# Where VectorE copies a pass's sums, in a cross-attention and expert kernel on one core

## The chip, the cores and the metric

The kernel runs on one core of one Trainium2 chip. The metric is the device time of one execution in microseconds (us), and the figure that is compared is the median over several runs. Five engines take part, each with its own in-order program: TensorE (PE in the rows, its weight loads PEld), VectorE (DVE), ScalarE (ACT), GpSimd (POOL) and SyncE (SP). They meet through semaphores: one instruction adds to a semaphore when it is done, and another engine's program waits until the semaphore has reached a number.

## The reference

Only the first half of the layer touches the change. `x` has 1024 tokens of 128 channels, `ctx` has 6404 rows of 96 channels, and there are 16 heads of 8 channels.

```python
q = layernorm(x) @ Wq + bq          # 1024 x 128
k = ctx @ Wk + bk;  v = ctx @ Wv + bv   # 6404 x 128
attn = softmax(clip(q_h @ k_h.T * scale))       # per head, 1024 x 6404
x = x + concat_h(attn @ v_h) @ Wo + bo
x = x + alpha * gelu(ln(x) @ W1m + b1m) @ W2m + (1 - alpha) * (two of eight experts, gated)
```

The softmax is taken without subtracting a maximum where a bound computed early in the kernel says that this is safe, and this branch is the one that runs.

## The kernel before, in words

**Passes and tiles.** The attention is cut into 8 passes. Pass `p` has 4 heads (`g`) and one half of the queries (512 of them). For every block of 128 context rows (`kt`, 0 to 49, and a short tail, 50) TensorE makes 4 score matmuls, one for each head, each 128 x 512 (L1143; the tail's is L1138). Three such chunks make a tile of 1536 columns in PSUM (`ps[t % 2]`), and ScalarE takes the exponential of a tile in one instruction (L533). There are 500 tiles. A finished block is multiplied with the values and a column of ones, and summed in a PSUM bank that the pass owns, `po[p % 2]` (L1228, the tail's L1214). Each of those 4 matmuls is two instructions in the trace, so a block is "x8" there.

**VectorE's share of the exponentials.** 27 blocks don't go to ScalarE. Their 108 chunks of scores go into the other bank, `po[1 - p % 2]`, as "spare jobs" of TensorE between two tiles (`spare_job`), at the tiles that `D_PLAN` names, and VectorE computes their exponential with a polynomial. For each chunk it runs L840 (round, into `du`) and L843 (the fraction, into `df`), which also frees the bank (`spare_taken`). For each pair of chunks it runs six steps, called stages in `pair_until`: stage 1 is L859, 2 is L868 (with a small L866 before it in some pairs), 3 is L870, 4 is L873, 5 is L876 and 6 is L879, which adds to `d_ready`. The stages of a pair run interleaved with the two chunks of the pair that follows: after the first of them up to stage 3, after the second up to stage 6. A block that is ready is summed at its own tile (the last number of a `D_PLAN` row).

**The end of a pass.** When the last block of pass `i` is summed, VectorE copies the bank to `oraw` (`take_sums`, L822; in the rows this is a COPY into region_kT, of which `oraw` is a part). A few tiles later TensorE transposes the copy, 4 blocks of 128 columns, back into the bank just freed: this is the spare job "tokens" (L1181). VectorE then normalises (`normalise`, L814 and L815) and adds to `spare_taken`. Every spare job waits until `spare_taken` has counted all jobs before it (L1159), so the chunk that follows "tokens" waits for `normalise`.

**What sets the order.** VectorE's program follows the list `SPARE`, the spare jobs in order of their tile. The "tokens" jobs stand at these tiles, with the score chunk ahead of each:

```
pass that ends   last tile   chunk before, its number and tile   tokens   next chunk
0                65          8 (first of its pair), 64           67       71
1                127         24 (first), 126                     130      133
2                190         40 (first), 189                     193      196
3                250         55 (second), 249                    252      256
4                312         71 (second), 311                    315      318
5                375         87 (second), 374                    378      381
6                436         102 (first), 431                    441      477
```

TensorE's order around a tile `t` is: scores of tile `t + 2` (which wait for the exponential of tile `t`), then the spare job of tile `t`, if there is one, then the values of the blocks that tile `t` completed.

Of the kernel before, what the change touches and what calls it, by code (L numbers as in the profile page):

```python
# [135 lines left out]
for gap in EPI_GAPS:  # L136
# [9 lines left out]
SPARE = sorted([(t, "score", GH * d + k) for d, (_, _, at, _, _) in enumerate(D_PLAN) for k, t in enumerate(at)]  # L146
               + [(NORM_AT[p], "tokens", p) for p in range(NP - 1)] + [(t, "v", c) for c, t in V_AT.items()]
               + [(t, "bound", n) for n, t in enumerate(BOUND_TILES)]
               + [(GSUM_TILE, "gsum", 0), (ROWS_TILE, "rows", 0)])
# [24 lines left out]
def pass_at(t):  # L174

    return min(p for p in range(NP) if t <= PASS_END[p])


def pv_bank(p):
    return p % 2  # L180
# [7 lines left out]
def build(nc, x, ctx, wq, bq, wk, bk, wv, bv, wo, bo, alpha, w_gate, b_gate, w1m, b1m, w2m, b2m,  # L188
# [4 lines left out]
    with ExitStack() as stack:  # L193
# [383 lines left out]
        def _(dve):  # L577
# [187 lines left out]
            def first_half_main(link):  # L765

                take_first_attT()
                residual(0, po[EPI_BANK][:, :], link)
                dve.wait_ge(std_ready, 2)
                scale_rows(halves[0])  # L770
                dve.wait_ge(xnT_psum, NHALF + 1)
                v.tensor_copy(xnT[:, 0:BANK], po[EPI_BANK][:, :]).then_inc(xnT_ready, 1)
                dve.wait_ge(xnT_ready, NHALF + 1)
                link(v.tensor_reduce(msum[:, 0:1], xnT[:, 0:BANK], AX.X, ALU.add))
                for cb in range(CB):
                    dve.wait_ge(pre_psum, cb + 1)
                    v.tensor_scalar(pre[:, cb, :], po[EPI_BANK][:, :], b1T[:, E * CB + cb:E * CB + cb + 1], None,  # L777
                                    ALU.add).then_inc(pre_taken, 1)
# [11 lines left out]
            with dve.If(safe != 0):  # L790
# [17 lines left out]
                def normalise(p, tok):  # L808

                    g, half = PASSES[p]  # L810
                    tok4 = tok.rearrange("p (t j m) -> p t j m", j=GH, m=QUAD)
                    tiles = slice(halves[half].start, halves[half].stop)
                    n = tiles.stop - tiles.start
                    flink(v.reciprocal(rden[:, tiles, :], tok4[:, :, :, D]))  # L814
                    return v.tensor_tensor(att_tok[:, tiles, g * GH * D:(g + 1) * GH * D].rearrange("p t (j d) -> p t j d", j=GH),  # L815
                                           tok4[:, :, :, 0:D],
                                           rden[:, tiles, :].unsqueeze(3).broadcast_to([P, n, GH, D]), ALU.mult)

                def take_sums(p):

                    dve.wait_ge(pv_done, VALUES_OF_PASS[p][-1] + 1)
                    v.tensor_copy(oraw[:, p % 2, :], po[pv_bank(p)][:, :]).then_inc(o_taken, 1)  # L822
# [5 lines left out]
                def d_count(key, ins):  # L828

                    d_done[0] += 1  # L830
                    d_mark[key] = d_done[0]
                    ins.then_inc(d_step, 1)

                def split_exponent(c, n):

                    i, m = divmod(c, 2)
                    part = slice(m * BANK, (m + 1) * BANK)
                    src = po[1 - pv_bank(pass_at(SPARE[n][0]))][:, :]
                    dve.wait_ge(spare_psum, n + 1)
                    d_count(("u", c), v.tensor_scalar(du[:, i % 2, part], src, MAGIC, None, ALU.add))  # L840
                    pair_until(i - 1, 1 + 3 * m)
                    dve.wait_ge(d_step, d_mark["u", c])
                    v.scalar_tensor_tensor(df[:, i % 2, part], du[:, i % 2, part], MAGIC, src,  # L843
                                           ALU.subtract, ALU.subtract).then_inc(spare_taken, 1)
                    pair_until(i - 1, 3 + 3 * m)

                def pair_until(i, stage):

                    if i < 0:
                        return  # L850
                    u, f, q = du[:, i % 2, :], df[:, i % 2, :], dq[:, :]
                    d, half = divmod(i, 2)
                    res = dres[:, d % 2, half * 2 * BANK:(half + 1) * 2 * BANK]
                    while d_stage[i] < stage:
                        d_stage[i] += 1
                        if d_stage[i] == 1:
                            dve.wait_ge(d_step, d_mark["u", 2 * i + 1])
                            dve.wait_ge(spare_taken, SPARE_OF["score", 2 * i + 1] + 1)
                            d_count(("e", i), v.tensor_scalar(u.bitcast(U32), u.bitcast(U32), 23, None, ALU.logical_shift_left))  # L859
                        elif d_stage[i] == 2:  # L860
                            if d >= 2:
                                dve.wait_ge(pv_done, VALUES_OF_D[d - 2] + 1)
                            if half == 0:
                                p, kt = D_PLAN[d][0:2]
                                heads = slice(GH * PASSES[p][0], GH * (PASSES[p][0] + 1))
                                v.tensor_scalar(vd[:, d % 2, :].rearrange("p (h m) -> p h m", m=V9), v9[:, kt, heads, :],  # L866
                                                C5, None, ALU.mult)
                            d_count(("q1", i), v.scalar_tensor_tensor(res, f, A1, f, ALU.add, ALU.mult))  # L868
                        elif d_stage[i] == 3:
                            d_count(("q2", i), v.scalar_tensor_tensor(q, f, A2, f, ALU.add, ALU.mult))  # L870
                        elif d_stage[i] == 4:
                            dve.wait_ge(d_step, max(d_mark["q1", i], d_mark["e", i]))
                            d_count(("p1", i), v.scalar_tensor_tensor(res, res, B1, u, ALU.add, ALU.mult))  # L873
                        elif d_stage[i] == 5:
                            dve.wait_ge(d_step, max(d_mark["p1", i], d_mark["q2", i]))
                            d_count(("p2", i), v.scalar_tensor_tensor(res, q, B2, res, ALU.add, ALU.mult))  # L876
                        else:
                            dve.wait_ge(d_step, d_mark["p2", i])
                            v.scalar_tensor_tensor(res, f, R0, res, ALU.subtract, ALU.mult).then_inc(d_ready, 1)  # L879

                pairs = 0
                for n, (_, kind, i) in enumerate(SPARE):
                    if n < JOBS_V:
                        continue
                    if kind == "score":
                        split_exponent(i, n)
                        pairs = (i + 1) // 2
                        if pairs == len(d_stage):
                            pair_until(pairs - 1, 6)
                    else:  # L890
                        take_sums(i)
                        if pairs:
                            pair_until(pairs - 1, min(6, d_stage[pairs - 1] + BETWEEN))
                        dve.wait_ge(spare_psum, n + 1)
                        ins = normalise(i, po[1 - pv_bank(i + 1)][:, :])
                        ins.then_inc(spare_taken, 1)
                        if i == LAST_OF_HALF[0]:
                            first_half_main(flink)
# [111 lines left out]
        def _(pe):  # L1010
# [80 lines left out]
            def ffn_sum(t):  # L1091

                n = max(n for n, (t0, _) in enumerate(OUT_TILES) if t0 <= t)
                a = t - OUT_TILES[n][0]
                return [po[0], po[1], bank(4)][n][:, a * P:(a + 1) * P], a == 0
# [93 lines left out]
            def values_step(n):  # L1189
# [11 lines left out]
                if first and p >= 1:  # L1201
                    used = sum(at <= t for at, _, _ in SPARE)
                    if used:
                        pe.wait_ge(spare_taken, used)
                    if p >= 2:
                        pe.wait_ge(o_taken, p - 1)
# [188 lines left out]
```

## Time and profile before

| | |
|---|---|
| median of three runs | 789.02 us (788.52 to 789.54) |
| profiled execution, its own time | 791.65 us |
| its span, first to last instruction | 789.7 us |
| granted TensorE clock, mean | 0.991 of full |
| TensorE matmuls busy | 735.0 us (93%) |
| ScalarE busy | 718.7 us (91%) |
| VectorE busy | 564.1 us (71%) |

The rows below come from one profiled execution, and their times are counted from the span's start. In a timeline row the first number is the start, the second is how long the instruction or the merged run of like instructions took, then engine, line, operation, output<-input, shapes and count; what stands in brackets is how long the engine had been idle before it and who released it. Starts of following rows may lie a little before the end of the row ahead, since consecutive instructions of an engine overlap.

### The profile page before, as it was taken

The page shows a single profiled execution, that of the slowest core. Times are in us where ns is not written, and L with a number is a line of the kernel's source. Part 1 is how long each engine was busy: PE and PEld are TensorE (multiplying, and loading weights), DVE is VectorE, ACT ScalarE, POOL GpSimd, SP SyncE. Part 2 cuts the span into 40 slices and gives each one's busy share as a digit, 9 for nine tenths or more (in the row PEclk, how much of TensorE's full clock was granted, in tenths as well). Part 3 has the DMA queues.
Part 4 walks back from the last instruction along what each step waited for, and adds up shares of the span by engine and source line. Part 5 has one row for each costly group of instructions (what it writes and reads, how often), then busy time and mean ns, then how long its engine had stood idle before and what let it go on. Part 6 is the DMA issues. An engine that isn't in the chain of part 4 may idle for free.

```text
span 789.7 us, 13292 instructions
## 1 busy us (share of the span) xinstructions
PE 735.0 (93%) x5412; PEld 219.5 (28%) x5412; DVE 564.1 (71%) x789; ACT 718.7 (91%) x574; POOL 28.8 (4%) x50
## 2 busy tenths in 40 slices
PE   6999989999999999999989999999999999999898
PEld 3534322222222222222222222222222222222457
DVE  6944278798878978797778897897879782139320
ACT  4868999999999999999989999999999999999351
POOL 5240000000000000000000000000000000000000
PEclk9979999999999999999999999999999999999999
DMA  4678000011110000111100000111100000000010
GB/s 163 196 184 260 25 1 1 23 46 34 34 34 1 2 1 1 34 49 36 51 1 2 1 1 18 34 38 48 34 1 1 1 1 1 2 1 1 2 54 27
DMA packets 18043, 28.53 MB, mean 36 GB/s; under 512 B 5286, under 2 KB 8732, under 8 KB 17980
## 3 DMA queue, kind: packets, MB, share of 16 engines
q1 hardware_dynamic: 12730, 23.71, 10.1%
q0 software_dynamic: 4032, 3.30, 1.8%
q8 instruction: 45, 0.74, 0.4%
q10 hardware_dynamic: 1218, 0.64, 0.3%
q14 instruction: 18, 0.15, 0.1%
HBM read 19.50 MB, written 8.13 MB: 35 GB/s over the span
## 4 chain that ended last, share of the span: by engine, by line
PE 57%; ACT 19%; issue 16%; DVE 4%; DMA 2%; POOLq 0%; SPq 0%; POOL 0%; ACTq 0%
PE po L1228 30%; PE ps L1143 16%; ACT region_ctx L533 14%; ACT probs_own L533 5%; PE ps L1323 2%; PE po L1044 2%; PE po L1333 1%; DMA k_dram<-kparts 1%; PE ps L1033 1%; PE po L1214 1%; DVE pT L632 1%; DMA xres<-in_x 1%; PE po L1143 1%; PE po L1120 1%; DMA region_ctx<-in_w1e 0%
## 5 line engine op out<-in xcount | busy, mean ns | idle before, releaser
L533 ACT ACTIVATE region_ctx<-ps 128x1536 f32<-128x1536 f32 x375 | 528.4, 1509 | 14.1 <-PE ps L1143 13.7
L1228 PE MATMUL po<-region_ctx,v 128*9 128x512 f32 x2238 | 392.8, 598 | 0.5 <-ACT region_ctx L533 0.5
L1143 PE MATMUL ps<-qst,region_k 32*128 32x512 f32 x1492 | 251.4, 494 | 36.2 <-ACT region_ctx L533 25.9
L1143 PEld LDWEIGHTS ps<-qst,region_k 32*128 32x128 f32 x1492 | 96.6, 182 | 408.9 <-ACT region_ctx L533 288.8
L1228 PE MATMUL po<-probs_own,v 128*9 128x512 f32 x746 | 193.8, 602 | 0.5 <-ACT region_ctx L533 0.5
L533 ACT ACTIVATE probs_own<-ps 128x1536 f32<-128x1536 f32 x125 | 188.7, 1509 | 4.2 <-PE ps L1143 3.8
L840 DVE TENSOR_SCALAR region_kT<-po 128x512 f32<-128x512 f32 x108 | 74.1, 686 | 90.5 <-PE po L1143 90.5
L843 DVE SCALAR_TENSOR_TENSOR region_kT<-region_kT,po 128x512 f32<-128x512 f32 x108 | 73.5, 680 | 0.3
L879 DVE SCALAR_TENSOR_TENSOR dres<-region_kT,dres 128x1024 f32<-128x1024 f32 x54 | 66.1, 1225 | 1.7
L876 DVE SCALAR_TENSOR_TENSOR dres<-region_kT,dres 128x1024 f32<-128x1024 f32 x54 | 65.8, 1218 | 0.2
L868 DVE SCALAR_TENSOR_TENSOR dres<-region_kT 128x1024 f32<-128x1024 f32 x54 | 65.7, 1217 | 0.0
L870 DVE SCALAR_TENSOR_TENSOR region_kT<-region_kT 128x1024 f32<-128x1024 f32 x54 | 65.7, 1217 | 0.0
L873 DVE SCALAR_TENSOR_TENSOR dres<-dres,region_kT 128x1024 f32<-128x1024 f32 x54 | 65.6, 1214 | 0.0
L1228 PEld LDWEIGHTS po<-region_ctx,v 128*9 128x9 f32 x2238 | 42.3, 88 | 69.7 <-issue 66.0
L1143 PE MATMUL po<-qst,region_k 32*128 32x512 f32 x108 | 51.4, 476 | 0.0
L859 DVE TENSOR_SCALAR region_kT<-region_kT 128x1024 uint32<-128x1024 uint32 x54 | 36.9, 683 | 0.0
L672 DVE COPY v<-po 128x512 f32<-128x512 f32 (+1 forms) x13 | 8.8, 680 | 30.8 <-PE po L1044 30.8
L1228 PE MATMUL po<-dres,vd 128*9 128x512 f32 x216 | 28.2, 595 | 0.0
L486 POOL TENSOR_TENSOR rstd<-rstd,powers 128x4 f32<-128x4 f32 x2 | 2.1, 1028 | 688.0 <-DVE rstd L604 688.0
L1228 PEld LDWEIGHTS po<-probs_own,v 128*9 128x9 f32 x746 | 19.7, 88 | 23.5 <-issue 22.2
L1143 PEld LDWEIGHTS po<-qst,region_k 32*128 32x128 f32 x108 | 19.6, 181 | 1.2 <-issue 1.2
L777 DVE TENSOR_SCALAR region_ctxT<-po,b1T 128x512 f32<-128x512 f32 x4 | 3.0, 750 | 19.2 <-PE po L1120 19.2
(216 smaller groups left out, 352.8 us busy)
## 6 DMA issues: line engine op xcount, KB each, us to landing
region_k<-k_dram SPq DMA_DIRECT2D x40, 320.0 KB, 3.3
k_dram<-kparts SPq DMA_DIRECT2D x18, 320.0 KB, 4.5
qst<-q_dram POOLq DMA_DIRECT2D x12, 128.0 KB, 9.6
region_ctx<-in_ctx SPq DMA_DIRECT2D x2, 624.0 KB, 9.7
q_dram<-dres POOLq DMA_DIRECT2D x2, 512.0 KB, 3.1
k_dram<-kparts SPq DMA_DIRECT2D x2, 322.0 KB, 3.5
region_ctx<-in_ctx SPq DMA_DIRECT2D x1, 576.0 KB, 8.1
xres<-in_x SPq DMA_DIRECT2D x1, 512.0 KB, 4.6
```

Source lines behind the costliest of these rows:

```text
L533: act.activation(probs_of(t), ps[t % NSB][:, :], ACT.Exp, scale=ESCALE).then_inc(exp_ready, 1)
L840: d_count(("u", c), v.tensor_scalar(du[:, i % 2, part], src, MAGIC, None, ALU.add))
L843: v.scalar_tensor_tensor(df[:, i % 2, part], du[:, i % 2, part], MAGIC, src, ALU.subtract, ALU.subtract).then_inc(spare_taken, 1)
L859: d_count(("e", i), v.tensor_scalar(u.bitcast(U32), u.bitcast(U32), 23, None, ALU.logical_shift_left))
L868: d_count(("q1", i), v.scalar_tensor_tensor(res, f, A1, f, ALU.add, ALU.mult))
L870: d_count(("q2", i), v.scalar_tensor_tensor(q, f, A2, f, ALU.add, ALU.mult))
L873: d_count(("p1", i), v.scalar_tensor_tensor(res, res, B1, u, ALU.add, ALU.mult))
L876: d_count(("p2", i), v.scalar_tensor_tensor(res, q, B2, res, ALU.add, ALU.mult))
L879: v.scalar_tensor_tensor(res, f, R0, res, ALU.subtract, ALU.mult).then_inc(d_ready, 1)
L1044: last = mm(dst[:, (t % 4) * P:(t % 4 + 1) * P], lhsT, wv_sb[:, :], start=True, stop=True)
L1143: return mm(dst, kst[r, kt * P:(kt + 1) * P], qst[r, g, queries], start=True, stop=True)
L1228: last = mm(dst[QUAD * j:QUAD * j + V9, :], w, src, start=first, stop=last_one, skip_group_check=True)
```

## The change

`take_sums(i)` is called when VectorE's program reaches the "tokens" entry of `SPARE`. Before, the stages that belong behind the last chunk ahead of it (`pair_until` at the end of `split_exponent`) have been issued by then. After, `split_exponent` returns ahead of that call where the next entry is "tokens", and the "tokens" branch makes the same call after `take_sums`. So the copy moves ahead of some stages:

```diff
                     v.scalar_tensor_tensor(df[:, i % 2, part], du[:, i % 2, part], MAGIC, src,
                                            ALU.subtract, ALU.subtract).then_inc(spare_taken, 1)
+                    if SPARE[n + 1:n + 2] and SPARE[n + 1][1] == "tokens":
+                        return
                     pair_until(i - 1, 3 + 3 * m)
...
                     else:
                         take_sums(i)
+                        if SPARE[n - 1][1] == "score":
+                            pair_until(SPARE[n - 1][2] // 2 - 1, 3 + 3 * (SPARE[n - 1][2] % 2))
                         if pairs:
                             pair_until(pairs - 1, min(6, d_stage[pairs - 1] + BETWEEN))
                         dve.wait_ge(spare_psum, n + 1)
```

Written out, VectorE's order from the chunk's L843 to `normalise`:

```
passes 0, 1, 2, 6   before  L843 L868 L870 copy L873 L876 normalise
                    after   L843 copy L868 L870 L873 L876 normalise
passes 3, 4, 5      before  L843 L876 L879 copy L859 L868 normalise
                    after   L843 copy L876 L879 L859 L868 normalise
```

No instruction is added or taken away, and no DMA, matmul or activation moves.

## Rows read from the trace of the kernel before

**Rows 1.** The page, busy time, share of the span and instructions of each engine

```profile
PE 735.0 (93%) x5412; PEld 219.5 (28%) x5412; DVE 564.1 (71%) x789; ACT 718.7 (91%) x574; POOL 28.8 (4%) x50
```

**Rows 2.** The copy's line L822, who waited for it: us, times

```profile
  PE po L1181: 1.8, 2
```

**Rows 3.** Timeline of VectorE at the end of pass 3

```profile
394.14 1.22 DVE L876 SCALAR_TENSOR_TENSOR dres<-region_kT,dres 128x1024 f32<-128x1024 f32 x1
...
396.54 0.68 DVE L822 COPY region_kT<-po 128x512 f32<-128x512 f32 x1
...
404.24 0.69 DVE L840 TENSOR_SCALAR region_kT<-po 128x512 f32<-128x512 f32 x1 [4.79 <-PE po L1143]
```

**Rows 4.** Timeline of TensorE at the end of pass 3

```profile
393.17 1.04 PE L1214 MATMUL po<-region_ctx,vtail 32*9 32x512 f32 x8
...
394.57 1.05 PE L1228 MATMUL po<-region_ctx,v 128*9 128x512 f32 x8
395.54 0.50 PE L1143 MATMUL ps<-qst,region_k 32*128 32x512 f32 x3
397.37 0.98 PE L1181 MATMUL po<-ident,region_kT 128*128 128x128 f32 x4 [1.32 <-DVE region_kT L822]
398.28 0.80 PE L1143 MATMUL ps<-qst,region_k 32*128 32x512 f32 x3
399.01 1.04 PE L1228 MATMUL po<-probs_own,v 128*9 128x512 f32 x3
...
400.84 0.52 PE L1143 MATMUL ps<-qst,region_k 32*128 32x512 f32 x3
...
404.40 0.50 PE L1143 MATMUL ps<-qst,region_k 32*128 32x512 f32 x3 [0.24 <-ACT region_ctx L533]
```

**Rows 5.** Timeline of ScalarE at the end of pass 3

```profile
394.68 2.87 ACT L533 ACTIVATE region_ctx<-ps 128x1536 f32<-128x1536 f32 x2 [0.30 <-PE ps L1143]
399.13 1.45 ACT L533 ACTIVATE region_ctx<-ps 128x1536 f32<-128x1536 f32 x1 [1.58 <-PE ps L1143]
401.41 1.45 ACT L533 ACTIVATE probs_own<-ps 128x1536 f32<-128x1536 f32 x1 [0.83 <-PE ps L1143]
402.81 4.19 ACT L533 ACTIVATE region_ctx<-ps 128x1536 f32<-128x1536 f32 x3
```

**Rows 6.** Windows: stretch, us, busy by engine, granted clock, DMA share, GB/s

```profile
398.00:400.00 2.00, 2.00 (x13) 0.42 (x11) 1.42 (x3) 0.87 (x1) 0.00 (x0) 0.50 0.04 8
```

**Rows 7.** Timeline of TensorE at the end of pass 1

```profile
229.71 0.63 PE L1181 MATMUL po<-ident,region_kT 128*128 128x128 f32 x4
```

**Rows 8.** Timeline of ScalarE at the end of pass 1

```profile
231.07 4.13 ACT L533 ACTIVATE region_ctx<-ps 128x1536 f32<-128x1536 f32 x3
```

**Rows 9.** Timeline of VectorE at the end of pass 0

```profile
141.29 1.22 DVE L868 SCALAR_TENSOR_TENSOR dres<-region_kT 128x1024 f32<-128x1024 f32 x1
...
143.56 0.68 DVE L822 COPY region_kT<-po 128x512 f32<-128x512 f32 x1
...
146.84 0.29 DVE L815 TENSOR_TENSOR xn<-po,rden 128x128 f32<-128x128 f32 x1
149.75 0.69 DVE L840 TENSOR_SCALAR region_kT<-po 128x512 f32<-128x512 f32 x1 [2.62 <-PE po L1143]
```

**Rows 10.** Timeline of TensorE after the end of pass 0

```profile
149.18 0.50 PE L1143 MATMUL po<-qst,region_k 32*128 32x512 f32 x1
149.91 0.50 PE L1143 MATMUL ps<-qst,region_k 32*128 32x512 f32 x3 [0.23 <-ACT probs_own L533]
...
154.56 1.05 PE L1228 MATMUL po<-dres,vd 128*9 128x512 f32 x8
```

**Rows 11.** Timeline of VectorE at the end of pass 6

```profile
649.55 0.69 DVE L822 COPY region_kT<-po 128x512 f32<-128x512 f32 x1 [2.77 <-PE po L1214]
...
651.41 1.23 DVE L876 SCALAR_TENSOR_TENSOR dres<-region_kT,dres 128x1024 f32<-128x1024 f32 x1
655.41 0.26 DVE L814 RECIPROCAL rden<-po 128x16 f32<-128x16 f32 x1 [2.77 <-PE po L1181]
```

## The prediction

> **What bounds the kernel now.** I read the page's first part, to see which engine could be the bound. TensorE is busy 93% of the span and ScalarE 91% [rows 1], so over most of the kernel they run in lockstep through the two score buffers, and VectorE, at 71%, matters only where one of them waits for it. So the second question is who waits for the copy that the change moves. The waits on its line say: TensorE's transposes, 1.8 us in two places [rows 2]. All that the change can remove directly is in those two places, and the timelines of the seven pass ends say where they are.
>
> One is the end of pass 3. TensorE finishes the pass's last sums with the tail block at 393.17 + 1.04 = 394.21 [rows 4]. VectorE at that time begins L876, then L879, and only then the copy, at 396.54 [rows 3]. TensorE has meanwhile summed a block of the next pass and made a tile of scores, and at 395.54 + 0.50 = 396.04 has nothing that it may do; it stands idle for 1.32 us, until 397.37 [rows 4]. What follows is the second thing to see: the transposes take 0.98 us there, against 0.63 at the end of pass 1 [rows 4, 7]; the next scores take 0.80 against 0.50, and the next block takes from 399.01 to 400.84, 1.83 us, against 394.57 to 395.54, 0.97 [rows 4]. The windows say why: the granted clock is 0.50 from 398 to 400, the lower of the two levels, 1.2 in place of 2.4 GHz [rows 6]. The engine had been idle for 1.32 us just before it fell. And ScalarE, the other half of the lockstep, stands idle for 1.58 and 0.83 us, waiting for scores [rows 5].
>
> The other place, with the remaining 1.8 - 1.32 = 0.48 us, is the end of pass 0, where the copy starts at 143.56 [rows 9]. I come to it below.
>
> **The change part by part. Pass 3.** L876 and L879 leave the path of the copy. It starts when L843 is done and the pass's sums are complete; L876 began at 394.14 and the sums were complete at 394.21, so I put the copy's start at 394.25 and its end 0.68 later, 394.93 [rows 3, 4]. TensorE comes to the transposes at 396.04, 1.1 us later, so its wait goes in full, with 1.1 us to spare.
>
> Now TensorE's own sum, up to the scores of 400.84: the wait 1.32, the transposes 0.98 - 0.63 = 0.35, the scores 0.80 - 0.50 = 0.30, the block 1.83 - 0.97 = 0.86 [rows 4, 7]. Together 2.83 us if the clock stays up, and 1.32 if it falls all the same.
>
> ScalarE may not let all of that through. Its natural step, start to start, follows from three exponentials in 4.13 us where it isn't kept waiting: (4.13 - 1.48) / 2 = 1.33 us, an estimate that takes 1.48 for the last one (a single one takes 1.45 here) [rows 5, 8]. The pair that starts at 394.68 ends at 397.55, so its second starts at 396.10; the third could follow at 397.43 and the fourth at 398.76. The fourth in fact starts at 401.41, so ScalarE gains 2.65 us [rows 5]. Would TensorE deliver in time? It starts the scores of the fourth at 400.84 - 2.83 = 398.01, and ScalarE begins 0.57 us after such a start (401.41 - 400.84), at 398.58, ahead of 398.76 [rows 4, 5]. So ScalarE's 2.65 is the smaller of the two, and I take it. The low end for this term is the idle time of ScalarE alone, 1.58 + 0.83 = 2.41, the high end TensorE's 2.83. At 404.40 TensorE is waiting for ScalarE again (0.24 us) [rows 4], which says that what ScalarE gains moves everything behind it.
>
> Does someone else take it back? L876 and L879 now run behind the copy, but the whole of VectorE's work up to `normalise` stays the same, with no wait in it, so `normalise` ends where it did, and VectorE then idles 4.79 us before the next chunk at 404.24 [rows 3]. That chunk comes 2.65 us earlier and still finds VectorE idle. The wait that was on the copy isn't replaced by one on VectorE; what is late next is TensorE, and then ScalarE.
>
> **Passes 1, 2, 4 and 5.** The transposes follow the scores ahead of them with at most about 0.1 us between, and ScalarE runs three exponentials in 4.13 us right behind, without a gap [rows 7, 8]; passes 2, 4 and 5 repeat this within a tenth. An earlier copy is worth between 0 and 0.1 us each; since ScalarE has no gap there I take 0. The moved stages run before `normalise` as they did.
>
> **Pass 0.** Here the change costs something. The copy starts at 143.56, right when the pass's sums complete, and L868 and L870 fill the time ahead of it, from 141.29 on [rows 9]. After, the copy can't start earlier, so the 0.48 us of TensorE stay, and VectorE stands waiting on the semaphore for 143.56 - 141.29 = 2.27 us, with L868, L870, L873, L876 and `normalise` queued behind. `normalise` ended at 146.84 + 0.29 = 147.13, so now at 149.40. The next chunk of scores waits for that. TensorE issued it at 149.18, so it comes 0.2 to 0.3 us late; but TensorE then idled 0.23 us waiting for ScalarE anyway [rows 10]. So of the 0.3 some 0.1 is left. The low end is 0, the high end the whole 0.3. VectorE's own 2.27 us fall into the 2.62 that it idled before 149.75 [rows 9]. The block that this VectorE work serves is summed at 154.56 [rows 10]; the last stage follows the chunk's two instructions, at 149.75 + 0.69 + 0.69, and takes 1.22 as the other stages do, so it ends by 152.4 [rows 3, 9], and 0.3 us doesn't reach the block.
>
> **Pass 6.** The copy already waits, 2.77 us, after L868 and L870 [rows 11]. After, those two run behind it: the last stage ended at 651.41 + 1.23 = 652.64, now 2.27 later, 654.91. `normalise` starts at 655.41, when the transposes are done [rows 11], so the cover left is 0.50 us, and I cost it at nothing. Without the cover each microsecond would go into the chain that turns the first half of the tokens into the next layer's input, not directly into the tiles.
>
> **Sum.** -2.65 (pass 3) + 0.1 (pass 0) = -2.55 us, with ends -2.83 - 0.4 = -3.2 (the three other passes and pass 1 with their 0.1 each, pass 0 at nothing) and -2.41 + 0.3 = -2.1. Against the profiled execution's own 791.65 us (its span is 789.7, and 1.95 lie around it) that is 789.1; its time stands 2.63 above the median of the runs shown. From the median, 789.02, I get 786.47, so 786.5.
>
> **The rivals. The clock didn't fall in the timed runs, or falls all the same (787.9).** The fall of the clock stands in one execution. If it is absent in the timed runs before, or present in those after, only the wait itself is gained: 1.32 us on TensorE; on ScalarE, whose third exponential would have started at about 397.37 + 0.63 + 0.57 = 398.57, against 397.43, 1.14. I take 1.2 between them, and 789.02 - 1.2 + 0.1 = 787.9. For it: the three times spread by 1.02 us, about what the fall costs (2.65 - 1.2 = 1.45), so some may have it and some not. Against it: the row shows the fall directly behind the longest stall of TensorE in this stretch, and the stall comes from program order, so every execution has it.
>
> The Trainium skill bears on this ("TensorE: Matmul & The Clock Gate", section "What's actually happening"): the activity window that decides the clock runs freely and doesn't begin with the kernel. By that rule the same stall drops the clock in some executions and not in others, and the sum would be anything between 787.9 and 786.5 as a median over runs; by the rows of the one profile it is 786.5. This trace shows one fall at one place and can't settle it.
>
> **Nothing comes of it (789.0).** Another wait takes the place of the copy's. The only candidates that I can name are VectorE, whose idle 4.79 us would have to be gone, or the lockstep giving the time back at the next tile without a block to sum. TensorE's wait for ScalarE at 404.40 speaks against the second.
>
> **Slower (791.0).** The mechanism is the waiting copy of pass 0: in-order VectorE holds `normalise`, that holds the chunk of tile 71, and this holds TensorE. The cover is 149.18 - 147.13 = 2.05 us against a delay of 2.27 [rows 9, 10]. Were the cover not there, all 2.27 would be a stall of TensorE, and a stall longer than pass 3's would bring a fall of the clock of its own, 1.45: together 3.7, less the 0.23 of rows 10, about 3.4; with only 1.2 to 1.4 gained in pass 3 the result is near 791.0. It decides only once `normalise` is later than 149.40 by more than about 2.5 us, for which I see no reason in the rows.
>
> **How the numbers follow.** The forecast has 0.58, with its own range of 785.8 to 787.1; the rival on the clock 0.22, spread from 787.2 to 788.2; nothing 0.11; slower 0.05; a gain beyond 3.1 us 0.04. The range reaches from 785.9 to 788.3, which leaves out some 2 in 10. A difference of 0.2%, 1.58 us, is about what the measurement can tell from no change; the line lies at 787.44. Faster by more takes the forecast nearly whole, the larger gains and a quarter of the clock rival: 0.65. Slower is 0.07 with a little of the "nothing" case, and 0.28 is left for the same.
>
> **What the profile after would show.** In pass 3, the copy about 0.6 us behind the start of L843, and TensorE's transposes directly behind the scores, at 0.63 us, with no idle time named for L822; the granted clock at its full level throughout that stretch; no idle ScalarE of over 0.3 us from the first exponential to the fourth. In pass 0, VectorE idle about 2.1 us ahead of the copy, `normalise` ending near 149.4, and the chunk behind it late by 0.2 to 0.3 us. In pass 6, `normalise` still released by the transposes. And passes 4 to 7 shifted as a whole by 2.5 us. The prediction is wrong if the fall of the clock turns up elsewhere, if it was absent in the timed runs, or if pass 0's late chunk shifts ScalarE by more than 0.3 us.

## The result and the profile after

After the change the median is 787.28 us (22 runs), against 788.87 us for the kernel before beside it (22 runs). The ratio is 0.9978 with a 95% interval of 0.9969 to 0.9987, so by this ratio the change saves 1.7 us, between 1.0 and 2.4; the two medians differ by 1.6. The forecast was 786.5 with a range of 785.9 to 788.3.

**Pass 3.** The profile of after has, in VectorE's timeline at the end of pass 3, the rows below. The added lines move the numbers of VectorE's stages by 2, so the L876 of before is L878 here.

```profile
393.23 0.68 DVE L843 SCALAR_TENSOR_TENSOR region_kT<-region_kT,po 128x512 f32<-128x512 f32 x1
393.96 0.69 DVE L822 COPY region_kT<-po 128x512 f32<-128x512 f32 x1
394.57 1.22 DVE L878 SCALAR_TENSOR_TENSOR dres<-region_kT,dres 128x1024 f32<-128x1024 f32 x1
...
398.99 0.29 DVE L815 TENSOR_TENSOR xn<-po,rden 128x128 f32<-128x128 f32 x1
401.05 0.69 DVE L840 TENSOR_SCALAR region_kT<-po 128x512 f32<-128x512 f32 x1 [1.77 <-PE po L1147]
```

TensorE in the same stretch (L1185 are the transposes, L1147 the scores, L1232 the sums; TensorE's numbers moved by 4):

```profile
395.24 0.50 PE L1147 MATMUL ps<-qst,region_k 32*128 32x512 f32 x3
395.67 0.66 PE L1185 MATMUL po<-ident,region_kT 128*128 128x128 f32 x4
396.25 0.50 PE L1147 MATMUL ps<-qst,region_k 32*128 32x512 f32 x3
396.69 0.61 PE L1232 MATMUL po<-probs_own,v 128*9 128x512 f32 x3
...
397.67 0.50 PE L1147 MATMUL ps<-qst,region_k 32*128 32x512 f32 x3
```

ScalarE:

```profile
394.37 4.21 ACT L533 ACTIVATE region_ctx<-ps 128x1536 f32<-128x1536 f32 x3 [0.31 <-PE ps L1147]
398.47 1.46 ACT L533 ACTIVATE probs_own<-ps 128x1536 f32<-128x1536 f32 x1
399.80 4.16 ACT L533 ACTIVATE region_ctx<-ps 128x1536 f32<-128x1536 f32 x3
```

And the windows, with the granted clock third from the end:

```profile
396.00:398.00 2.00, 2.00 (x17) 0.58 (x15) 2.00 (x3) 2.00 (x2) 0.00 (x0) 1.00 0.04 8
```

The copy is 0.73 us behind the start of L843, where it was 2.4 us behind the start of L876, which followed L843 directly [rows 3]. The transposes follow the scores with no idle time and take 0.66 us, not 0.98; the block behind them takes 397.67 - 396.69 = 0.98 us, not 1.83 [rows 4]. The clock stays at the upper level, where it was at the lower one [rows 6], and ScalarE's idle times of 1.58 and 0.83 us are gone [rows 5].

**Pass 0.** Here the profile after is not what was forecast. VectorE:

```profile
140.75 0.68 DVE L843 SCALAR_TENSOR_TENSOR region_kT<-region_kT,po 128x512 f32<-128x512 f32 x1
142.19 0.69 DVE L822 COPY region_kT<-po 128x512 f32<-128x512 f32 x1 [0.76 <-PE po L1218]
...
147.75 0.29 DVE L815 TENSOR_TENSOR xn<-po,rden 128x128 f32<-128x128 f32 x1
149.28 0.69 DVE L840 TENSOR_SCALAR region_kT<-po 128x512 f32<-128x512 f32 x1 [1.25 <-PE po L1147]
```

TensorE (L1218 is the tail block, the last of the pass):

```profile
141.08 1.04 PE L1218 MATMUL po<-region_ctx,vtail 32*9 32x512 f32 x8
142.06 0.50 PE L1147 MATMUL ps<-qst,region_k 32*128 32x512 f32 x3
142.49 1.04 PE L1232 MATMUL po<-region_ctx,v 128*9 128x512 f32 x8
143.47 0.51 PE L1147 MATMUL ps<-qst,region_k 32*128 32x512 f32 x3
143.90 0.66 PE L1185 MATMUL po<-ident,region_kT 128*128 128x128 f32 x4
```

VectorE waits only 0.76 us, not 2.27. The pass's sums are complete with the tail block at 141.08 + 1.04 = 142.12; what TensorE sums at 142.49 belongs to the next pass. So the copy comes 1.4 us earlier, TensorE's wait of 0.48 us is gone too, and `normalise` ends at 147.75 + 0.29 = 148.04. The rows at the pass's end in the profile of before, which neither the prediction nor the rows ahead of it show, have the same order:

```profile
141.03 1.04 PE L1214 MATMUL po<-region_ctx,vtail 32*9 32x512 f32 x8
142.00 0.50 PE L1143 MATMUL ps<-qst,region_k 32*128 32x512 f32 x3
142.43 1.05 PE L1228 MATMUL po<-region_ctx,v 128*9 128x512 f32 x8
```

**Pass 6**, VectorE: the wait of 2.77 us [rows 11] has grown, as the stages L866, L868 and L870 (numbers of before) now stand behind it, and 0.41 us of cover are left ahead of `normalise`, which the transposes still release.

```profile
646.48 0.69 DVE L822 COPY region_kT<-po 128x512 f32<-128x512 f32 x1 [5.13 <-PE po L1218]
...
652.34 0.26 DVE L814 RECIPROCAL rden<-po 128x16 f32<-128x16 f32 x1 [0.41 <-PE po L1185]
```

**A measure that leaves out the start.** The start of the kernel varies from execution to execution by several microseconds (below), which hides a difference of this size. So I compare executions over a stretch that the change doesn't shift at either end: from TensorE's first matmul on a block of VectorE's (`dres`, tile 56) to its last (tile 499). The tile view of `dres` gives both; before, then after:

```profile
L1228 PE MATMUL po<-dres,vd x216: 592/595/598, 127.8 to 736.0; 128*9 128x512 f32 x108
```

```profile
L1232 PE MATMUL po<-dres,vd x216: 592/595/598, 127.8 to 732.9; 128*9 128x512 f32 x108
```

That is 608.2 us before and 605.1 after. Counted from that first matmul, the exponential of a given tile is 0.33 to 0.43 us earlier from tile 76 to tile 254, and 3.1 us earlier from tile 258 on, and nothing changes behind that. So this one pair of executions says 3.1 us, more than the 2.55 forecast, while the timed runs say 1.7. The experiments had to find out why.

### The profile page after: what moved, and what is told of

The parts are those of the page before. It is cut to its first block, busy times and chain, and to the rows that moved or that the text cites. A ratio compares the mean times of both kernels' runs of the same rounds, so it can differ in the third digit from the quotient of the medians.

```text
span 786.9 us, 13292 instructions
## 1 busy us (share of the span) xinstructions
PE 733.3 (93%) x5412; PEld 219.2 (28%) x5412; DVE 564.5 (72%) x789; ACT 718.1 (91%) x574; POOL 28.8 (4%) x50
## 4 chain that ended last, share of the span: by engine, by line
PE 58%; ACT 19%; issue 16%; DVE 3%; DMA 2%; POOLq 0%; SPq 0%; POOL 0%; ACTq 0%
PE po L1232 31%; PE ps L1147 17%; ACT region_ctx L533 14%; ACT probs_own L533 5%; PE ps L1327 2%; PE po L1048 2%; DMA k_dram<-kparts 1%; PE po L1337 1%; PE po L1218 1%; PE ps L1037 1%; DVE pT L632 1%; PE po L1147 1%; DMA xres<-in_x 1%; PE po L1124 1%; DMA region_ctx<-in_w1e 0%
## 5 line engine op out<-in xcount | busy, mean ns | idle before, releaser
L1232 PE MATMUL po<-region_ctx,v 128*9 128x512 f32 x2238 | 392.0, 598 | 0.5 <-ACT region_ctx L533 0.5
L1147 PE MATMUL ps<-qst,region_k 32*128 32x512 f32 x1492 | 251.1, 493 | 36.6 <-ACT region_ctx L533 26.3
L1147 PEld LDWEIGHTS ps<-qst,region_k 32*128 32x128 f32 x1492 | 96.5, 182 | 408.3 <-ACT region_ctx L533 289.9
L1232 PE MATMUL po<-probs_own,v 128*9 128x512 f32 x746 | 192.9, 598 | 0.5 <-ACT region_ctx L533 0.5
L843 DVE SCALAR_TENSOR_TENSOR region_kT<-region_kT,po 128x512 f32<-128x512 f32 x108 | 73.5, 680 | 0.3
L878 DVE SCALAR_TENSOR_TENSOR dres<-region_kT,dres 128x1024 f32<-128x1024 f32 x54 | 65.8, 1218 | 0.2
L870 DVE SCALAR_TENSOR_TENSOR dres<-region_kT 128x1024 f32<-128x1024 f32 x54 | 65.8, 1218 | 0.0
L1232 PEld LDWEIGHTS po<-region_ctx,v 128*9 128x9 f32 x2238 | 42.3, 88 | 69.8 <-issue 66.1
L1147 PE MATMUL po<-qst,region_k 32*128 32x512 f32 x108 | 51.5, 476 | 0.0
L1232 PE MATMUL po<-dres,vd 128*9 128x512 f32 x216 | 28.2, 595 | 0.0
L1232 PEld LDWEIGHTS po<-probs_own,v 128*9 128x9 f32 x746 | 19.7, 88 | 23.3 <-issue 22.0
L1147 PEld LDWEIGHTS po<-qst,region_k 32*128 32x128 f32 x108 | 19.6, 181 | 1.2 <-issue 1.0
```

Of the source, the lines that this page charges most:

```text
L1147: return mm(dst, kst[r, kt * P:(kt + 1) * P], qst[r, g, queries], start=True, stop=True)
L1232: last = mm(dst[QUAD * j:QUAD * j + V9, :], w, src, start=first, stop=last_one, skip_group_check=True)
```

## The experiments

Theory A: the stall of pass 3 is in every execution of before, but the clock falls behind it in only some of them. Theory B: the fall is there each time, and the other pass ends give back what is missing. In the edits `MOVED` is the set of passes in which the copy moves.

**Pass 3 alone (e1) and all but pass 3 (e2).**

```diff
-                    if SPARE[n + 1:n + 2] and SPARE[n + 1][1] == "tokens":
+                    if SPARE[n + 1:n + 2] and SPARE[n + 1][1] == "tokens" and SPARE[n + 1][2] in MOVED:
                         return
...
-                        if SPARE[n - 1][1] == "score":
+                        if SPARE[n - 1][1] == "score" and i in MOVED:
```

with `MOVED = (3,)` in e1 and `(0, 1, 2, 4, 5, 6)` in e2.

> The copy moves ahead of the stages at the end of pass 3 alone. Theory A (the other pass ends cost nothing; in pass 3 the stall is worth 1.2 us in every execution and the fall of the clock 1.45 more, but only in the executions that have it): the same time as the whole change, 787.3 us, to within 0.3. Theory B (each execution gains 2.65 us in pass 3, and the other pass ends lose about 1 us again): 786.3 us, clearly under the whole change. In the profile of either: no wait of TensorE on the copy in pass 3, full clock there, and the 0.48 us wait of pass 0 as before.

Measured: 787.61 us, ratio 0.9978 (0.9963 to 0.9993), or 1.7 us less (0.6 to 2.9), which holds what either theory expected. The tile view of `dres` gives 605.6 us, 2.6 less than the first profile of before:

```profile
L1233 PE MATMUL po<-dres,vd x216: 592/595/599, 125.8 to 731.4; 128*9 128x512 f32 x108
```

> The copy moves in passes 0, 1, 2, 4, 5 and 6 but not in pass 3. Theory A: as before, 788.9 us, at most 0.3 above. Theory B: about 1 us above before, 789.9 us. In the profile: TensorE's wait of 1.32 us on the copy in pass 3 is still there; the chunk behind pass 0's normalise is 0.2 to 0.3 us late; whether the clock falls in pass 3 is open by theory A and certain by theory B.

Measured: 788.21 us, ratio 0.9985 (0.9971 to 0.9999). The time fell, where theory B expected about 1 us more. The same view gives 607.9 us; the timeline of TensorE in pass 3 has the stall and the slow clock:

```profile
L1233 PE MATMUL po<-dres,vd x216: 592/595/598, 122.7 to 730.6; 128*9 128x512 f32 x108
```

```profile
391.99 0.63 PE L1186 MATMUL po<-ident,region_kT 128*128 128x128 f32 x4 [1.30 <-DVE region_kT L823]
392.54 0.50 PE L1148 MATMUL ps<-qst,region_k 32*128 32x512 f32 x3
...
394.58 0.80 PE L1148 MATMUL ps<-qst,region_k 32*128 32x512 f32 x3
```

Against the first profile of before, 608.2 us, the other pass ends lose nothing; they gain 0.3 us. That tells against theory B's second half. The chunk behind pass 0 was expected late in e2, and it wasn't.

**Four more executions of before (e4, e8, e9, e10).** The same kernel, five traces with the first.

> The kernel before once more, for its clock. Theory A: the stall of 1.32 us at the end of pass 3 is there again, and the fall behind it may be there or not; without it the scores and the block behind the transposes take 0.50 and 0.97 us, and ScalarE's idle times of 1.58 and 0.83 us shrink to about 1.1 us together. Theory B: stall and fall both there.

> One more look at before, for the clock in pass 3. The stall of 1.3 us is there by all theories; theory A: with a fall behind it or without; theory B: with it.

> Another look at before, for the share of executions in which the clock falls behind pass 3's stall. So far, of five traces with the stall of 1.3 us, three have the fall and two have it not. With a share of 0.6 this one has it more likely than not; with 0.2, which the medians of the timed runs point to, most likely not. Where it falls, tile 258 and all behind it come 1.55 us later than where it doesn't.

> The same once more: fall or no fall in pass 3, with 1.55 us between the two from tile 258 on and nothing in between.

e4 has the fall. TensorE's timeline:

```profile
396.40 0.63 PE L1181 MATMUL po<-ident,region_kT 128*128 128x128 f32 x4 [1.31 <-DVE region_kT L822]
396.96 0.51 PE L1143 MATMUL ps<-qst,region_k 32*128 32x512 f32 x3
...
398.84 0.80 PE L1143 MATMUL ps<-qst,region_k 32*128 32x512 f32 x3
```

e8 has the same stall and no fall. TensorE, then ScalarE, then the window:

```profile
395.46 0.63 PE L1181 MATMUL po<-ident,region_kT 128*128 128x128 f32 x4 [1.32 <-DVE region_kT L822]
396.02 0.50 PE L1143 MATMUL ps<-qst,region_k 32*128 32x512 f32 x3
...
397.43 0.50 PE L1143 MATMUL ps<-qst,region_k 32*128 32x512 f32 x3
```

```profile
396.57 1.45 ACT L533 ACTIVATE region_ctx<-ps 128x1536 f32<-128x1536 f32 x1 [0.93 <-PE ps L1143]
397.98 1.45 ACT L533 ACTIVATE probs_own<-ps 128x1536 f32<-128x1536 f32 x1
```

```profile
396.00:398.00 2.00, 2.00 (x19) 0.61 (x22) 1.51 (x3) 1.43 (x2) 0.00 (x0) 1.00 0.04 8
```

The view of `dres`, for e4 and for e8:

```profile
L1228 PE MATMUL po<-dres,vd x216: 592/595/599, 126.8 to 735.1; 128*9 128x512 f32 x108
```

```profile
L1228 PE MATMUL po<-dres,vd x216: 592/595/598, 125.9 to 732.6; 128*9 128x512 f32 x108
```

That is 608.3 us with the fall and 606.7 without. e9 (606.6 us) and e10 (606.7 us) have no fall in pass 3 either. There is nothing in between, as expected: tile 258 and all behind it stand 1.5 to 1.6 us earlier in the three executions without the fall. In e8 ScalarE is idle behind the stall once, for 0.93 us, and not for 1.58 and 0.83 [rows 5]. In none of the twelve traces here does the granted clock fall anywhere else between the first and the last block of VectorE's, and TensorE's other idle times in that stretch are 0.8 us at most.

One thing these traces can't separate. The two falls behind a stall of 1.3 us in the experiments (e2, e4) are from one chip, number 12, and the four traces without (e6, e8 on chip 3; e9, e10 on chip 2) from two others; the first profile's chip isn't known. So the share of executions with the fall may differ from chip to chip, and that it changes between two executions on the same chip isn't shown. The medians of before on chips 12 and 3, 788.83 and 789.04 us, don't show chip 12 slower by a fall, but the start of the kernel varies enough to hide it.

**The copy moved in pass 0 alone (e6)**, `MOVED = (0,)`.

> The copy moves ahead of L868 and L870 in pass 0 alone. From the traces of e2 and of the whole change, whose tiles behind pass 0 stand 0.35 to 0.43 us earlier: the same shift here, 0.37 us, and none at any later pass end; time 0.4 us under before, which the spread of the runs may hide. By the prediction's cost it would be 0.1 us later. In pass 3 the stall of 1.3 us is there, and the fall of the clock with it in some executions by theory A, in each by theory B.

Measured: 788.86 us, ratio 1.0004 (0.9987 to 1.0020), which can't tell 0.4 us. The trace can: 606.4 us in the view of `dres`, and from tile 76 to tile 254 each exponential is 0.34 to 0.42 us earlier than before. In pass 3 the stall of 1.32 us is there, without a fall:

```profile
L1233 PE MATMUL po<-dres,vd x216: 592/595/598, 124.5 to 730.9; 128*9 128x512 f32 x108
```

```profile
393.77 0.63 PE L1186 MATMUL po<-ident,region_kT 128*128 128x128 f32 x4 [1.32 <-DVE region_kT L823]
```

**TensorE kept busy in the stall (e3, e5).** Both put four matmuls with zero weights ahead of the wait; they add zeros to the running sums of pass 4. e3 uses a new tile `zero9` that GpSimd clears early in the kernel, e5 the zeros that `vtail` has beside its blocks:

```diff
                 elif kind == "tokens":
+                    if i == 3:
+                        for j in range(GH):
+                            r = slice(QUAD * ((j + 1) % GH), QUAD * ((j + 1) % GH + 1))
+                            mm(po[pv_bank(4)][QUAD * j:QUAD * j + V9, :], vtail[r, 0, QUAD * j:QUAD * j + V9],
+                               xnT[r, 0:BANK], start=False, stop=False, skip_group_check=True)
                     pe.wait_ge(o_taken, i + 1)
```

> Before, with one block's worth of matmuls (4, by a zero weight of 9 columns, so that they add zeros to the running sums) put ahead of TensorE's wait for the copy of pass 3: TensorE is busy for about 1.0 us of its 1.32 us stall, and nothing else changes. If the stall is what drops the clock: the clock stays full through pass 3, the stretch behind it runs at the full step, and of the 2.65 us the 1.45 us of the clock are regained in executions that had the fall: 787.5 us if nearly all have it, 788.2 us if about half do. If the clock falls for another reason: 788.9 us and a fall in the profile as before. A fall that is seldom there in the timed runs also gives 788.9 us, but with none in the profile.

Measured: 789.35 us, ratio 1.0001 (0.9987 to 1.0016). In the profile TensorE, then the view of `dres`:

```profile
396.96 1.05 PE L1184 MATMUL po<-xnT,zero 128*9 128x512 f32 x8
398.25 0.66 PE L1189 MATMUL po<-ident,region_kT 128*128 128x128 f32 x4 [0.25 <-DVE region_kT L824]
```

```profile
L1236 PE MATMUL po<-dres,vd x216: 592/595/598, 128.7 to 735.4; 128*9 128x512 f32 x108
```

> As e3 (zero matmuls in TensorE's stall of pass 3), but with zeros that are there already, so that the start of the kernel is left as it was. Theory A, the fall of the clock behind the stall is there in only some executions: the tiles behind pass 3 come 1.55 us earlier than in an execution of before that has the fall and level with one that has it not, no fall in pass 3 in the profile, and the median falls by 1.55 us times the share of executions with the fall, 0.3 to 1.0 us. Theory B, every execution of before has the fall: 1.5 us under before in the median as well.

Measured: 788.82 us, ratio 0.9995 (0.9973 to 1.0016); 606.6 us in the view of `dres`, and no fall in pass 3. So both stand at 606.6 to 606.7 us, level with the executions of before that have no fall, as theory A has it: busy or idle, the 1.3 us on the path are the same, and with TensorE idle the fall comes on top in some. Two traces alone don't show that filling the stall keeps the clock up, since four of seven with the stall have no fall either. Neither median fell clearly. e3's interval of -1.0 to +1.3 us leaves out the 1.4 us of nearly every execution having the fall and holds the 0.7 of about half. Its profile has another fall of the clock early, near 67 us, and whether the added clearing changes the start isn't settled: the first block, at 128.7, lies within the 123.0 to 129.2 of before. e5's interval of -2.1 to +1.3 us holds what either theory expected.

**A longer stall (e7).**

```diff
+                        if i == 3:
+                            pair_until(pairs - 1, 2)
                         take_sums(i)
-                        if pairs:
+                        if pairs and i != 3:
```

> Before, with L859 and L868 of the next pair also put ahead of the copy in pass 3, so that it comes 1.73 us later and TensorE's stall grows from 1.3 to about 3.1 us. If the clock fall is tied to the stall, it is there in each execution now. Theory B: 1.7 to 1.8 us above before, for the stall alone, since before had the fall each time. Theory A: that plus what the fall costs in the executions that had none before: 2.3 us above with a share of 0.6, 2.9 with 0.2.

Measured: 792.21 us, ratio 1.0044 (1.0024 to 1.0063), or 3.5 us above before (1.9 to 5.0). TensorE and the view of `dres`:

```profile
397.82 0.63 PE L1183 MATMUL po<-ident,region_kT 128*128 128x128 f32 x4 [3.06 <-DVE region_kT L822]
...
400.82 0.80 PE L1145 MATMUL ps<-qst,region_k 32*128 32x512 f32 x3
```

```profile
L1230 PE MATMUL po<-dres,vd x216: 592/595/599, 126.5 to 736.5; 128*9 128x512 f32 x108
```

That is 610.0 us: 1.8 above the executions of before with the fall, and 3.3 above those without. The fall is in this one trace; that it is in every timed execution of e7 is assumed. If so, the excess of 3.5 suggests that most timed executions of before are of the second kind, though the interval's low end, 1.9, nearly admits the first.

## Why the prediction was right, and where not

**Pass 3, the stall.** Right, as placed and nearly as sized. Without the stall, transposes, scores and blocks follow each other at full step. Against an execution of before with the fall the gain is 2.66 us (e1's exponentials against the first profile's), where the prediction had 2.65. The split between its two parts is: with the stall bridged or no fall (e3, e8), 1.55 us less than with the fall; so the stall itself is worth 1.1 us and the fall 1.55. The views of `dres` say the same of the stall: 606.7 us in e8 and 605.6 in e1. The rival on the clock had 1.2 and 1.45.

**The fall as a thing of every execution.** This is the step that failed. The prediction took one profile's fall as given, and its sentence "the stall comes from program order, so every execution has it" is true of the stall and not of the fall. Of the seven traces that have the stall of 1.3 us, three show the fall (the first, e2, e4) and four don't (e6, e8, e9, e10). The traces without such a stall (after, e1, e3, e5) show none there. These counts alone are small; what ties the fall to the stall is that each fall of that stretch, e7's too, begins at most 1.5 us behind it, and that this stretch has no other fall. With three in seven the expected gain is 1.1 + 0.4 + 1.55 x 3/7 = 2.2 us, inside the measured 1.0 to 2.4; with a fall in each execution it would be 3.1, outside. So the rival on the clock had the right mechanism for four traces of seven. The Trainium skill's sentence that was set beside it ("TensorE: Matmul & The Clock Gate", section "What's actually happening": the activity window runs freely and doesn't begin with the kernel) fits e4 and e8, where stalls of 1.31 and 1.32 us end in a fall and in none; that the window is the reason, and not the chip, no trace shows. The exact share stays open. Three in seven gives 2.2 us for the change and 3.3 - 1.55 x 3/7 = 2.6 for e7; measured are 1.7 and 3.5, which would fit a share near nothing better, and both intervals hold three in seven too. The prediction had named a fall "absent in the timed runs" as a sign of being wrong, and four traces of seven point that way.

**Pass 0.** Wrong in sign, a reading error. The prediction put the completion of the sums at 143.56, where the block of 142.43 + 1.05 = 143.48 ends, and took that block for the last of pass 0. The tail block L1214 is the last one, as it had itself read for pass 3, and it ended at 141.03 + 1.04 = 142.07, 1.4 us earlier; L868 and L870 didn't fill a wait, they held the copy up. So VectorE's wait was 0.76 us and not 2.27, `normalise` was 0.9 us later and not 2.27, the chunk behind it wasn't late, and the wait of 0.48 us that was said to stay went. Forecast +0.1 us, measured -0.33 to -0.43 (after, e6).

**Passes 1, 2, 4 and 5 at nothing.** Right: between tile 76 and tile 254, and from tile 258 to the end, the distance between before and after stays within 0.1 us, and e2 and e6 both have gained the same 0.34 to 0.35 us at tile 254, the one with and the other without passes 1 and 2.

**Pass 6 at nothing.** Right: the cover was 0.41 us, of the 0.50 worked out; the stages behind the copy include L866, which the sum had left out.

**The sum.** The term for pass 3 was too large by the 1.55 us of the fall in four of seven executions, about 0.9 us on average, and the term for pass 0 too small by 0.5. The two errors offset each other in part: 2.55 forecast, some 2.2 by the traces, 1.7 (1.0 to 2.4) by the timed runs. So part of the hit is luck. The measured 787.28 lies in the stated range of 785.9 to 788.3, but the prediction's own split gave its forecast 785.8 to 787.1 and the rival on the clock 787.2 to 788.2, and it is the rival's part that it falls into. Without the 0.4 us that pass 0 gave where a loss was forecast it would lie at about 787.7. The slower rival's mechanism never came near: `normalise` of pass 0 ended at 148.04, not 149.40.

## What to carry to other kernels

A copy that another engine waits for belongs ahead of work that nobody waits for yet, but only where the data is there when the copy is reached: look up, for each place, which instruction really completes it, since at the seam of two passes the next pass's work is already running. When a stall in a profile is followed by a slow clock, price the two apart, and read a second and third trace, on more than one chip, before counting on the clock. And where the start of a kernel varies by more than the effect, compare traces between two instructions that the change leaves alone.

## What the runs showed of the hardware

**The start.** These are the span and the mean clock of the kernel before in e9, then in e10, each with its window of 38 to 60 us:

```profile
core 0: 783.8 us, clock 1.000
```

```profile
38.00:60.00 22.00, 20.51 (x153) 8.30 (x153) 12.35 (x27) 17.84 (x14) 9.26 (x21) 1.00 0.83 237
```

```profile
core 0: 789.8 us, clock 0.991
```

```profile
38.00:60.00 22.00, 20.34 (x117) 7.57 (x119) 11.32 (x23) 14.20 (x11) 9.35 (x21) 0.77 0.79 200
```

Their 6 us of difference are made by the time of VectorE's first block, which is summed at 123.0 in e9 and at 129.2 in e10; from there on they take 606.6 and 606.7 us. In e9 the clock doesn't fall at all; in e10 it is at the lower level for about 10 us between 40 and 51 us, and for 3.4 us more between 19 and 24, and TensorE issues 117 matmuls in that window where it issues 153 in e9. Over the twelve traces the first block goes with the time at the lower level ahead of it: 122.7 and 123.0 without any (e2, e9), 124.5 with about 3 us (e6), 125.8 to 126.8 with about 7 (e1, e4, e5, e7, e8), 127.8 to 128.7 with about 10 (the first profile, after, e3), 129.2 with about 14 (e10). In this kernel the start moves the time of an execution by over three times what the change does.

**The rest is steady.** Of the traces of before, between the first block and the last there are just two lengths, 606.6 to 606.7 and 608.2 to 608.3 us, told apart by one fall of the clock.

**A short stall.** A stall of TensorE of 1.3 us had a fall of the clock behind it in three of seven traces; the fall began between 0.1 and 1.5 us behind the end of the stall (the first profile and e4), and the clock was at the lower level for 3.4 us each time. Where four matmuls filled 1.05 us of the stall (e3, e5), there was none, in two traces.
